# A two-stage expert-routing kernel on one core: the second expert's first gather is issued ahead of the tails' gathers, the first tail moves into the first set of turned rows, one wait of the tensor engine goes, and one unread indirect transfer is added at the start

## The reference, cut to what matters

```python
x = x + _L0_ffn_ref(_L0_cond_ref(x, ...), gate_w, expert_w)   # the stage of this change
x = x + _L1_ffn_ref(_L1_cond_ref(x, ...), weight, lora_A, lora_B, ...)

def _L0_ffn_ref(x, gate_w, expert_w):
    logits = jnp.einsum('bsh,he->bse', x, gate_w)
    topv, topi = jax.lax.top_k(logits, TOP_K)          # TOP_K = 2 of 8
    w = jax.nn.softmax(topv, axis=-1)
    onehot = jax.nn.one_hot(topi, E, dtype=x.dtype)
    w_e = jnp.einsum('bske,bsk->bse', onehot, w)
    out = jnp.einsum('bsh,eho,bse->bso', x, expert_w, w_e)
```

## Time and profile before

| | |
|---|---|
| median of 3 runs | 806.38 us (802.54 to 806.95) |
| the profiled execution: its own time, and its span | 804.94 us, 803.2 us |
| PE busy | 781.4 us, 97% of the span |
| DVE, ACT, POOL busy | 392.4, 206.4, 85.0 us |
| share of the chain that ended last | PE 85%, DVE 5%, DMA 5%, issue 2% |

### The profile page before, as it was taken

One profiled execution on the slowest core, in us unless ns is written; L12 is line 12 of the kernel. 1 busy time (PEld: TensorE's weight loads), 2 busy tenths in 40 slices (PEclk: granted clock), 3 DMA queues, 4 the chain that ended last, 5 costly groups with the idle time before them and its releaser, 6 DMA issues.

```text
span 803.2 us, 13018 instructions
## 1 busy us (share of the span) xinstructions
PE 781.4 (97%) x4426; PEld 635.9 (79%) x4426; DVE 392.4 (49%) x920; ACT 206.4 (26%) x324; POOL 85.0 (11%) x127
## 2 busy tenths in 40 slices
PE   6999898899999999999999999999999999999997
PEld 4565687678787787877878888888988889889886
DVE  2598551231412303214133153476777667778883
ACT  3445151241513314224133251301000010001200
POOL 1000212001110110101011012311111111200000
PEclk9999999999999999999999999999999999999999
DMA  9997496376482765726355255774445554442065
GB/s 347 385 377 293 126 381 228 121 253 242 171 320 98 246 253 194 278 97 230 143 188 189 101 197 176 242 193 112 104 111 143 144 125 104 114 99 51 1 230 189
DMA packets 62880, 152.51 MB, mean 190 GB/s; under 512 B 7148, under 2 KB 24700, under 8 KB 61948
## 3 DMA queue, kind: packets, MB, share of 16 engines
q1 hardware_dynamic: 43152, 99.84, 38.0%
q0 software_dynamic: 9504, 34.48, 14.0%
q10 hardware_dynamic: 10188, 17.71, 5.9%
HBM read 99.04 MB, written 44.57 MB: 179 GB/s over the span
## 4 chain that ended last, share of the span: by engine, by line
PE 85%; DVE 5%; DMA 5%; issue 2%; ACT 1%; SPq 1%; POOLq 0%; POOL 0%; ACTq 0%; DVEq 0%
PE bank L1501 61%; PE bank L1606 6%; PE bank L1615 4%; PE bank L1492 4%; PE bank L1561 3%; PE bank L1622 3%; DMA work<-c_scratch,idx 3%; DVE weights L1026 1%; PE bank L1393 1%; PE bank L1572 1%; DVE work L991 1%; DMA work<-y_scratch,pos_c 1%; DMA x1p<-res 1%; PE bank L1356 1%; DVE work L990 1%
## 5 line engine op out<-in xcount | busy, mean ns | idle before, releaser
L1501 PE MATMUL bank<-weights,l_hi 128*128 128x512 f32 x1520 | 468.7, 389 | 0.0
L1501 PEld LDWEIGHTS bank<-weights,l_hi 128*128 128x128 f32 x1520 | 285.4, 188 | 57.6
L1501 PE MATMUL bank<-weights,l_lo 128*128 128x512 f32 x760 | 301.6, 397 | 0.0
L1501 PEld LDWEIGHTS bank<-weights,l_lo 128*128 128x128 f32 x760 | 142.7, 188 | 32.5 <-issue 4.9
L1086 DVE TENSOR_TENSOR l_lo<-bank,l_hi 128x512 fp32r<-128x512 f32 x32 | 22.1, 692 | 175.8 <-ACT l_hi L797 167.8
L1118 DVE TENSOR_TENSOR weights<-work,weights 128x1024 fp32r<-128x1024 f32 x48 | 55.9, 1219 | 33.9 <-ACT weights L809 33.9
L1606 PE MATMUL bank<-conv_sb,x1p 128*128 128x128 f32 x512 | 59.8, 275 | 2.1 <-DMA x1p<-work 1.1
L1606 PEld LDWEIGHTS bank<-conv_sb,x1p 128*128 128x128 f32 x512 | 58.7, 192 | 2.6 <-DMA x1p<-work 1.3
L1240 DVE TENSOR_TENSOR res<-bank,res 128x512 f32 (+1 forms) x30 | 31.9, 1063 | 54.2 <-PE bank L1501 43.2
L648 POOL DMA_INDIRECT work<-c_scratch,idx x32 | 33.5, 1048 | 222.5 <-PE bank L1492 136.4
L888 ACT ACTIVATE l_hi<-work 128x512 fp32r<-128x512 f32 x32 | 18.4, 623 | 135.2 <-PE bank L1501 129.1
(11 more groups left out here) (208 smaller groups left out, 616.7 us busy)
## 6 DMA issues: line engine op xcount, KB each, us to landing
work<-in_expert_w SPq DMA_DIRECT2D x52, 512.0 KB, 6.1
y_scratch<-work ACTq DMA_DIRECT2D x64, 256.0 KB
x1p<-in_expert_w SPq DMA_DIRECT2D x20, 512.0 KB, 7.9
y_scratch<-ca SPq DMA_DIRECT2D x19, 512.0 KB
res<-in_x SPq DMA_DIRECT2D x16, 512.0 KB, 11.7
c_scratch<-work SPq DMA_DIRECT2D x16, 512.0 KB, 5.1
res<-in_x_ph SPq DMA_DIRECT2D x14, 512.0 KB
x1p<-res SPq DMA_DIRECT2D x112, 64.0 KB
```

Source lines behind the costliest of these rows:

```text
L1501: mm = pe.matmul(to[:, :], a[:, k, :], b[:, k, cols * HALF:(cols + 1) * HALF], start=(k == 0 and n == 0), stop=(k == HC - 1 and n == 2 and ...
```

## The change

It has three parts. POOL fetches expert 1's first slot ahead of the two tails' gathers. Expert 0's tail moves from the last place of the second set of turned rows to the first place of the first set, so that `first_tail` waits for two copies in place of four; the other two are waited for at expert 5's tail, the first one in the second set; and the tail of expert 2 no longer waits for the eviction of expert 0's tail, which is in another bank. At the start POOL does an indirect transfer of 128 times 64 bytes into a tile that nothing reads, and waits for it.

```diff
-TAILED = [2, 3, 4, 5, 6, 7, 0]
+TAILED = [0, 2, 3, 4, 5, 6, 7]
...
+        unread = sb("unread", [P, 16])[:, :]
...
             pool.memset(cumf[:, 0:1], 0.0).then_inc(s_init, 1)
+            pool.memset(pos_c[0][:, :], 0).then_inc(s_pool0, 1)
+            pool.wait_ge(s_pool0, 1)
+            pool.indirect_dma_start(unread, None, x.rearrange("n (a b) -> (n a) b", b=16),
+                                    bass.IndirectOffsetOnAxis(ap=pos_c[0][:, 0:1], axis=0)).then_inc(s_unread, 16)
+            pool.wait_ge(s_unread, 16)
...
-            def fetch_slots(e, start):
+            def fetch_slots(e, start, end=None):
...
-                with pool.Fori(start, count) as t:
+                with pool.Fori(start, count if end is None else end) as t:
...
             with pool.Fori(0, 1) as e:
                 fetch_slots(e, 1)
+            with pool.Fori(1, 2) as e:
+                fetch_slots(e, 0, 1)
             pool.wait_ge(s_lo, 2 * HC)
             pool.wait_ge(s_tidx, 16 * QUAD)
             for j in range(2):
                 rows = min(GROUPED - j * QUAD, QUAD) * TAIL
                 pool.indirect_dma_start(tail_x[j][0:rows, :], None, c0_d,
                                         bass.IndirectOffsetOnAxis(ap=tail_idx[0:rows, j:j + 1], axis=0)).then_inc(s_tgot[j], 16)
-            with pool.Fori(1, E) as e:
+            with pool.Fori(1, 2) as e:
+                fetch_slots(e, 1)
+            with pool.Fori(2, E) as e:
                 fetch_slots(e, 0)
...
-                dve.tensor_copy(to[:, 0, :], tail_f[:, 2:2 + QUAD]).then_inc(s_tplace, 1)
-                dve.tensor_copy(to[:, 1, 0:2], tail_f[:, 2 + QUAD:E]).then_inc(s_tplace, 1)
-                dve.tensor_copy(to[:, 1, 2:3], tail_f[:, 0:1]).then_inc(s_tplace, 1)
+                dve.tensor_copy(to[:, 0, 0:1], tail_f[:, 0:1]).then_inc(s_tplace, 1)
+                dve.tensor_copy(to[:, 0, 1:QUAD], tail_f[:, 2:1 + QUAD]).then_inc(s_tplace, 1)
+                dve.tensor_copy(to[:, 1, 0:GROUPED - QUAD], tail_f[:, 1 + QUAD:E]).then_inc(s_tplace, 1)
...
             def tail(e, half):
-                if half == 0:
+                if half == 0 and e > 2:
                     pe.wait_ge(s_tev, e - 1)
+                if half == 0 and TAILED.index(e) == QUAD:
+                    for taken in s_txt[2:]:
+                        pe.wait_ge(taken, 1)
...
             def first_tail():
-                for taken in s_txt:
+                for taken in s_txt[0:2]:
                     pe.wait_ge(taken, 1)
```

More of the change, by code:

```diff
@@ L382, in build @@
         s_out = sem("s_out")
+        s_pool0 = sem("s_pool0")
+        s_unread = sem("s_unread")
         tile_rows = lambda t: bass.ds(t * P, P)
```

## The result

The changed kernel takes 800.98 us (median of 12 runs, 799.47 to 803.15), the kernel before 804.90 (12 runs beside it). The ratio is 0.9946, with a 95% interval of 0.9927 to 0.9965: 2.8 to 5.9 us faster, where 3.45 was forecast. The profiled execution took 802.44 us, with a span of 800.7 against 803.2.

What follows compares the result with a forecast made beforehand. TensorE, busy for nearly the whole span, was taken as the bound, so only its waits count. Gains of 2.36 + 0.39 + 0.70 + 0 = 3.45 us gave 802.5 us, range 799.5 to 806.3.

Steps and rivals of the forecast that it cites:

- Part 1: Expert 1's first slot gathered ahead of the tails' gathers: TensorE's wait before slot 4's transposes goes, 2.36 us gained.
- (b): Wait handed on: slot 4's gather or the tails' land late, keeping 0.5 to 2.4 us of the gain; chance 0.18.
- (d): Slower: TensorE comes to wait for the tails' gathers, which undo the whole gain if landing after 141.25 us; chance 0.05.
- Part 2: First tail waits for two copies in place of four, so TensorE starts it earlier: 0.39 us gained.
- Part 3: Next tail no longer waits for the eviction of the first tail: 0.70 us gained, 0.49 at the least.
- Part 4: Early unread transfer at the start, ahead of the first gather: taken as 0 us, with 1.03 as the other end.
- Rival (c): First gather, ahead of slot 0, gets shorter by 1.03 us, making the gain 4.48 us; chance 0.13.
- The sum: Gains over the whole kernel: 2.36 + 0.39 + 0.70 + 0 = 3.45 us, or 0.43%.
- The time: Whole kernel forecast at 802.5 us, between 801.5 off the profiled execution and 802.9 off the median.
- Faster or the same: Whole kernel against a line of about 0.5%, 4.03 us: chances faster 0.34, same 0.63, slower 0.03.
- Case (a): The summed gain holds for the whole kernel: 3.2 to 3.7 us, giving 801.2 to 803.2 us; chance 0.64.

## Why the prediction was right, and where it was not

- **Part 1, 2.36 us:** measured as forecast, 11.77 or 11.78 us in each of the nine profiles with the early fetch. The tails' gathers landed in 4.8 to 5.2 us where I had taken 6, so no part of the wait was handed on; rivals (b) and (d) did not come about.
- **Part 2, 0.39 us:** 0.58. I had kept the 0.25 us between ACT's copy and PE's start; with the last copy no longer waited for, PE starts 0.05 us behind the first (137.45 + 0.60 = 138.05, and 138.10). Why it is 0.05 and not 0.25 is not shown.
- **Part 3, 0.70 us:** 0.65 or 0.66, from 7.61 to 6.96, in six of eight profiles without the eviction wait. In two of them, the changed kernel's own among them, 0.5 and 1.3 us of idle or slowed products stood there. That I had not listed: I took for certain that PE, released earlier, would find its work there.
- **Part 4, nothing:** 0.15 us at the gather, not to be seen in time. Rival (c) is refuted by the kernel in which a first call without DVE beside it lasts 1.08 us. 2.00 us beside the subtraction and 1.08 without agree with what the Trainium skill states in "SBUF — State Buffer", section "Who interferes with whom": a DVE instruction with two SBUF inputs contends with a GpSimd instruction that reads SBUF. The Trainium skill's 6 us in "GPSIMD Engine Reference", section "Instruction dispatch", are for the first call of freshly loaded code. An indirect transfer's first call here costs 0.14 us, so they do not apply to it; no run here measures the loading of code.
- **The sum, 3.45 us:** the parts measured at their marks give 2.36 + 0.58 + 0.65 + 0.15 = 3.74. Among executions whose mean clock is 0.999 or more, the changed kernel's 20 (two sets, medians 800.98 and 800.90) are 2.9 to 3.0 us below the 41 of the kernel before (median 803.87). Over all executions the medians of before and changed differ by 3.9 to 4.4 us (804.90 in its own set, 805.43 over 99). The difference is put down to the clock: 58 of 99 executions against 4 of 24, at 3.0 us, are 1.3 us on the average, and 2.9 + 1.3 = 4.2. The sum priced the wait at its idle time and left out that PE's clock may fall behind it. That 3.45 came so near to the measured 3.9 is therefore partly luck: at full clock less was measured, and a term that was not in the sum made it up. Whether the 0.8 us between 3.74 and 2.9 are real is open. Resampling the 61 executions gives 2.3 to 3.6 us as the 95% interval of the 2.9 (an estimate), which holds 3.45 and just misses 3.74. The prediction said that nothing ahead up to 505 us could take time back. But in five of the nine profiles with the early fetch, and in none of the other four, PE waits 0.17 to 0.42 us for a late gather at about 471 us; this is the changed kernel's second profile:

```profile
471.40 1.10 PE L1506 MATMUL bank<-ca,work 128*128 128x128 f32 x8 [0.36 <-DMA work<-c_scratch,idx]
```

- **The time, 802.5 us:** measured 800.98. It was reckoned from a start of 805.95, halfway between the profiled execution and a median of 3; the 12 executions beside the changed kernel have 804.90. That is 1.05 of the 1.5 us, and the larger gain the other 0.5.
- **Faster or the same:** I had "within 0.5%" as the likeliest and the estimate is 0.54%, with an interval on both sides of the line. Case (a) stood 0.3 to 0.8 us short of it; by the estimate above the clock is what carried it over.

That executions with a lower mean clock become rarer when the wait for slot 4's gather goes is shown by the counts. That the idle time itself brings the drop is argued, from two profiles in which it falls right behind a wait of 1.9 to 2.0 us; a kernel that keeps the wait and fills it with products was not tried.

The kernel without the unread transfer and with the later subtraction had the lowest ratio, 0.9939 (0.9913 to 0.9964). It is 0.9 us ahead of the changed kernel at its mark, and in time not to be told from it.

## What to carry to other kernels

Order the queue that issues indirect transfers by when each result is wanted, and look first at whether the moved ones then fly under a lighter DMA load; here they took 5 us in place of 9, with a DMA share of 0.68 over their flight in place of 1.01. Price a wait of TensorE by its idle time and by the granted clock behind it, over many executions: single profiles differed by 1 to 3 us at places that the change does not touch. Before a first call is warmed up, see what VectorE does beside it.

## What was not expected of the hardware

- The first products of the kernel ran at different speeds: four of them took 1.96 us in six profiles, and 2.90 to 3.76 in seven, around 21 to 25 us. In the kernel before, four transposes just ahead took 1.12 us and the same four behind 0.60, which looks like the clock's step from one level to the other. The column of the granted clock shows 1.00 there, but the trace's own list of granted clocks has no entry for the first stretch. It begins at 23.1 us in the kernel before and at 21.0 in the changed one, where the products get short, and at 15.5 to 25.9 us over the thirteen profiles. The later it begins, the later the row numbers are written, 79.6 us at one end and 82.8 at the other. So executions can differ by some 3 us before the experts' stage, as much as this change is worth, and the mean granted clock does not show it. The list has no lower entry for that stretch, so that it is the clock is still argued.
- One more wait ahead of a gather shifted its start from 0.28 to 0.75 us behind its releaser, without a VectorE subtraction beside it too.
- PE stood still for 0.35 and 0.91 us where a packet of the instruction queue was 3.8 and 4.5 us behind the first tail's start.
